# Four groups of expert tiles, late norms on VectorE, five result buffers, and the experts' first layer as three fp32r products

## What is computed

```python
x = x + tanh(g_xattn[1]) * attention16(layernorm(x), ctx)
xf = layernorm(x)                       # 2048 tokens x 128
gates = xf @ gate_w + gate_b            # 8 experts
scores, idx = top_k(gates, 2); g = softmax(scores)
for each expert e:                      # w1: 128 x 512, w2: 512 x 128
    y = gelu(xf @ w1[e] + b1[e]) @ w2[e] + b2[e]
    out += g_e * y                      # only where e is among a token's two
x = x + tanh(g_ffn[1]) * out
```

## Time and profile before

| | |
|---|---|
| median of 3 runs | 412.39 us (411.47 to 415.35) |
| profiled execution, its own time | 412.65 us |
| its span, first to last instruction | 410.9 us |
| TensorE busy (matmul) | 307.9 us, 75% |
| VectorE busy | 265.3 us, 65% |
| ScalarE busy | 198.1 us, 48% |
| GpSimd busy | 162.6 us, 40% |

### The profile page before, as it was taken

The page is one execution under the profiler, slowest core; times in us unless marked ns, Lnnn a source line. Parts: engine busy times, 40 slices in busy tenths (PEclk is TensorE's granted clock), DMA queues, the critical chain, the costliest instruction groups (busy, mean ns, idle before and its releaser), DMA issues.

```text
span 410.9 us, 7400 instructions
## 1 busy us (share of the span) xinstructions
PE 307.9 (75%) x2316; PEld 250.3 (61%) x2317; DVE 265.3 (65%) x878; ACT 198.1 (48%) x395; POOL 162.6 (40%) x289
## 2 busy tenths in 40 slices
PE   1568785271476999999999999995498999999300
PEld 0457774210333787877877787664398999999300
DVE  4647887498983978978979797855274323232162
ACT  1136664454923667666566666563153544454100
POOL 4350111450552401215272644633627644554432
PEclk9959999575557799999999999998699999999855
DMA  7434672554010111101110111005536878874171
GB/s 196 150 128 180 241 274 46 69 86 109 1 38 2 24 32 24 25 22 46 37 46 21 49 27 40 21 8 172 178 101 203 259 227 246 233 219 137 47 247 51
DMA packets 30618, 43.76 MB, mean 106 GB/s; under 512 B 5075, under 2 KB 24086, under 8 KB 30198
## 3 DMA queue, kind: packets, MB, share of 16 engines
q1 hardware_dynamic: 25798, 35.71, 30.1%
q0 software_dynamic: 3008, 6.23, 4.8%
q10 hardware_dynamic: 1776, 1.38, 1.1%
HBM read 21.99 MB, written 15.01 MB: 90 GB/s over the span
## 4 chain that ended last, share of the span: by engine, by line
PE 63%; DVE 11%; DMA 8%; issue 7%; POOL 6%; ACT 2%; DVEq 0%; SPq 0%; POOLq 0%
PE bank L1419 57%; DMA k_all<-k_hi 3%; DVE x L1390 2%; POOL k_all L315 2%; DVE nmax L1172 1%; PE bank L1734 1%; DMA xg<-sorted_rows 1%; DMA y_in<-y_rows 1%; DVE xn L919 1%; DMA sorted_rows<-token_row,place 1%; PE bank L1667 1%; POOL x L547 1%; PE bank L1445 1%; DMA x<-in_x 1%; PE bank L1679 1%
## 5 line engine op out<-in xcount | busy, mean ns | idle before, releaser
L837 ACT ACTIVATE probs<-bank 128x512 f32<-128x512 f32 x128 | 71.0, 597 | 43.9 <-PE bank L1419 43.7
L1172 DVE TENSOR_REDUCE nmax<-bank 128x2 f32<-128x512 f32 x128 | 81.7, 678 | 4.4 <-PE bank L1419 3.7
L848 ACT ACTIVATE hid<-bank,wbuf 128x256 f32<-128x256 f32 x92 | 39.6, 475 | 52.7 <-PE bank L1419 52.7
L657 POOL DMA_INDIRECT y_rows<-yout,to_row x46 | 44.0, 957 | 39.3 <-DVE yout L1379 31.4
L1419 PE MATMUL bank<-q_st,k_quad 128*128 128x256 f32 x256 | 56.0, 308 | 0.8 <-ACT probs L837 0.7
L1419 PE MATMUL bank<-k_quad,q_st 128*128 128x256 f32 x256 | 53.7, 296 | 1.6 <-ACT q_st L800 0.7
L1419 PE MATMUL bank<-xg_t,wbuf 128*128 128x256 f32 x184 | 45.3, 390 | 2.4 <-issue 1.8
L1419 PEld LDWEIGHTS bank<-q_st,k_quad 128*128 128x128 f32 x256 | 38.7, 193 | 11.9 <-ACT probs L837 11.2
L1419 PE MATMUL bank<-wbuf,hid 128*128 128x128 f32 x368 | 45.0, 275 | 0.5 <-DVE yout L1379 0.5
L1419 PEld LDWEIGHTS bank<-wbuf,hid 128*128 128x128 f32 x368 | 43.0, 192 | 0.8 <-DVE yout L1379 0.7
L1419 PEld LDWEIGHTS bank<-k_quad,q_st 128*128 128x128 f32 x256 | 40.5, 196 | 3.9 <-DVE nmax L1172 2.2
(11 more groups left out here) (237 smaller groups left out, 589.4 us busy)
## 6 DMA issues: line engine op xcount, KB each, us to landing
wbuf<-in_moe_pack SPq DMA_DIRECT2D x23, 578.0 KB, 4.1
sorted_rows<-zeros SPq DMA_DIRECT2D x15, 572.0 KB, 4.1
k_quad<-k_all SPq DMA_DIRECT2D x64, 48.0 KB
xg<-sorted_rows SPq DMA_DIRECT2D x23, 132.0 KB, 3.5
ctx_in<-in_ctx SPq DMA_DIRECT2D x8, 128.0 KB, 2.8
x<-in_x SPq DMA_DIRECT2D x4, 256.0 KB, 5.1
k_all<-k_hi SPq DMA_DIRECT2D x16, 64.0 KB
k_all<-k_lo SPq DMA_DIRECT2D x16, 64.0 KB
```

The lines of the kernel that those rows point to most:

```text
L657: pool.indirect_dma_start(out=y_rows[:, :], out_offset=bass.IndirectOffsetOnAxis(ap=to_row[n % 4][:, i:i + 1], axis=0), in_=yout[n % 3][:, ...
L837: act.activation(probs[quad % 2][:, j, :, :], bank[2 + j % 2][:, :] .rearrange("p (r s) -> p r s", r=2), ACT.Exp, scale=SC1)\
L848: act.activation(hid[n % 2][:, ch, :], bank[ch][:, 0:SLOT], ACT.Gelu, bias=wbuf[n % WB][:, B1P + ch:B1P + ch + 1]).then_inc(sem("gelued"), 1)
L1172: dve.tensor_reduce(nmax[m.par][:, gp, qt, :, j], bank[QUERY_BANKS[u % 3]][:, :].rearrange("p (r s) -> p r s", r=2), AX.X, ALU.max, negate ...
```

## The change

`PHASES` becomes four groups: three tiles after batch 4, two after batch 5, two after batch 6, 16 after batch 7. The buffers for weights, tokens and names move into the memory that is live during the attention, and the loads of the first three tiles no longer wait for the last attention. Tile 0 is turned at k = 1 of step 8 and goes through its first layer at k = 4; tiles 1 and 2 follow at k = 10, then the second layer of tile 0. VectorE takes the tokens of tile 0 at k = 2, those of tiles 1 and 2 at k = 12, weighs tile 0, and plans the third group there; the first planning moves to k = 6 of step 7.

The last norms, of batches 6 and 7, move to VectorE (`late_norm`, at k = 11); GpSimd keeps only names and root for them, and in its last round sorts batch 6 ahead of that. There are five buffers for results and seven for names instead of three and four.

The first layer's f32 product becomes three fp32r products per chunk: high weights by high tokens, high weights by low tokens, low weights by high tokens. ScalarE makes the high weights (`split_w1`), VectorE the low weights and both halves of the tokens (`take_tokens`).

```diff
-PHASES = ((0, 5), (5, 2), (7, NT - 7))
-KNOWN = (BATCH - 3, BATCH - 2, BATCH - 1)
+YB = 5
+PHASES = ((0, 3), (3, 2), (5, 2), (7, NT - 7))
+KNOWN = (BATCH - 4, BATCH - 3, BATCH - 2, BATCH - 1)
...
+        wbuf = [sb(f"wbuf{i}", [P, PACK], scope=c) for i in range(WB)]
...
-        xg_t = [sb(f"xg_t{i}", [P, SLOT], scope=d) for i in range(2)]
+        xg_hi = [sb(f"xg_hi{i}", [P, SLOT], F32R, d) for i in range(2)]
+        xg_lo = [sb(f"xg_lo{i}", [P, SLOT], F32R, d) for i in range(2)]
+        w1_hi = [sb(f"w1_hi{i}", [P, HID], F32R, d) for i in range(2)]
+        w1_lo = [sb(f"w1_lo{i}", [P, HID], F32R, d) for i in range(2)]
         hid = [sb(f"hid{i}", [P, HC, SLOT], scope=d) for i in range(2)]
...
-            sp.wait_ge(sem("attended"), 4 * BATCH)
+            first = PHASES[1][0]
             sp.wait_ge(sem("tiles_set"), 2)
-            for n in range(WB):
+            for n in range(first):
                 load_weights(n)
-            for i in range(2):
-                sp.wait_ge(sem(f"rows_sorted{i}"), 64 * 3)
...
+            sp.wait_ge(sem("rows_sorted0"), 64 * 3)
+            sp.wait_ge(sem("rows_sorted1"), 64 * 2)
+            for n in range(first):
                 load_rows(n)
-            for n in range(4, NT):
+            for n in range(first, NT):
                 if n == PHASES[1][0]:
                     sp.wait_ge(sem("tiles_set"), 4)
-                    sp.wait_ge(sem("rows_sorted2"), 64)
+                    sp.wait_ge(sem("rows_sorted1"), 64 * 3)
                 if n == PHASES[2][0]:
                     sp.wait_ge(sem("tiles_set"), 6)
+                    sp.wait_ge(sem("rows_sorted2"), 64)
...
             def fourth_norm(b):
+                if b.n >= BATCH - 2:
+                    pool.wait_ge(sem(f"rows_sorted{(b.n - 3) % 2}"), 64 * ((b.n - 3) // 2 + 1))
+                    pool.tensor_copy(token_row[b.n % 3][:, :, :, DM], row_no[:, 2 * b.n:2 * b.n + 2, :])\
+                        .then_inc(sem("rows_named"), 1)
+                    rstd_of(b.n + (LN4 + 1), mv[b.par], var_eps[b.par], rstd[b.par], 2)
+                    return
                 rows_b = token_row[b.n % 3]
...
                 pool.wait_ge(sem("placed"), b + 1)
-                pool.wait_ge(sem("rows_named"), 2 * b + 2)
+                late = max(0, b - (BATCH - 3))
+                pool.wait_ge(sem("rows_named"), 2 * b + 2 - late)
+                if late:
+                    pool.wait_ge(sem("xn4_copied"), late)
                 pool.wait_ge(sem("xn4_ready"), b + 1)
...
                 if 2 <= n < BATCH:
                     choose(pool, n - 2)
+                if n == BATCH:
+                    sort_rows(n - 2)
                 fourth_norm(Step(0, n - 1, BATCH))
-                if n >= 2:
+                if 2 <= n < BATCH:
                     sort_rows(n - 2)
...
                     if is_step(s, BATCH) and k == 4:
                         act.activation(gelu_first[:, :], eps[:, 0:1], ACT.Gelu)
+                        split_w1(0)
+                    if is_step(s, BATCH) and k == 5:
+                        split_w1(1)
+                        gelu_tile(0)
                     if is_step(s, BATCH) and k == 15:
-                        gelu_tile(0)
+                        split_w1(2)
+                        gelu_tile(1)
...
+            def split_w1(n):
+
+                act.wait_ge(sem(f"w_landed{n % WB}"), 16 * (n // WB + 1))
+                if n >= 2:
+                    act.wait_ge(sem("hid_done"), HC * (n - 1))
+                act.activation(w1_hi[n % 2][:, :], wbuf[n % WB][:, 0:HID], ACT.Copy).then_inc(sem("w1_high"), 1)
...
             unrolled(step_c, BATCH)
-            for n in range(1, NT):
+            for n in range(2, NT):
+                if n + 1 < NT:
+                    split_w1(n + 1)
...
                         halves_of(o.par, 2, o.n * SEQ)
                     if o.valid and k == 11:
                         variances_of(o.n + (LN4 + 1), o.par, 2)
+                        if is_step(o, BATCH - 2) or is_step(o, BATCH - 1):
+                            late_norm(o.n)
                     if s.valid and s.n >= 2 and k == 3:
                         top_two(s.n - 2)
                     if s.valid and s.n >= 2 and k == 13:
                         find_place(s.n - 2, bank[7])
+                    if is_step(s, BATCH - 1) and k == 6:
+                        begin_tiles(0)
                     if is_step(s, BATCH - 1) and k == 14:
-                        begin_tiles(0)
+                        begin_tiles(1)
+                    if is_step(s, BATCH) and k == 2:
+                        take_tokens(0)
                     if is_step(s, BATCH) and k == 12:
-                        take_tokens(0)
                         take_tokens(1)
-                        begin_tiles(1)
+                        take_tokens(2)
+                        weigh(0)
...
                         maximum(k - QUERY_LAG)
+
+            def late_norm(b):
+
+                late = b - (BATCH - 3)
+                dve.wait_ge(sem("rstd_done"), b + (LN4 + 1))
+                dve.wait_ge(sem("rows_named"), 2 * b + 2 - late)
+                for k, ready in ((0, "xn4_ready"), (1, "xn4_copied")):
+                    for i in range(2):
+                        ins = norm(token_row[b % 3][:, i, k, 0:DM], x[:, b * SEQ + i * P:b * SEQ + (i + 1) * P], b % 2, i)
+                    ins.then_inc(sem(ready), 1)
             def add_gate_bias(b, raw):
...
                 dve.wait_ge(sem("xg_turned"), n + 1)
                 if n >= 2:
                     dve.wait_ge(sem("hid_done"), HC * (n - 1))
-                dve.tensor_copy(xg_t[n % 2][:, :], bank[6][:, 0:SLOT]).then_inc(sem("xg_t_ready"), 1)
+                dve.tensor_copy(xg_hi[n % 2][:, :], bank[6][:, 0:SLOT]).then_inc(sem("xg_split"), 1)
+                dve.wait_ge(sem("w1_high"), n + 1)
+                dve.tensor_tensor(w1_lo[n % 2][:, :], wbuf[n % WB][:, 0:HID], w1_hi[n % 2][:, :].bitcast(F32),
+                                  ALU.subtract)
+                dve.wait_ge(sem("xg_split"), n + 1)
+                dve.tensor_tensor(xg_lo[n % 2][:, :], bank[6][:, 0:SLOT], xg_hi[n % 2][:, :].bitcast(F32),
+                                  ALU.subtract).then_inc(sem("xg_t_ready"), 1)
                 names = xg[n % 4][:, :, DM]
                 dve.scalar_tensor_tensor(spare[n % 2][:, :], names, 0.5, spare_no[:, n, :], ALU.is_lt, ALU.mult)\
...
             unrolled(step_c, BATCH)
-            for n in range(NT):
+            add_gate_bias(BATCH - 1, bank[4][:, 0:16])
+            top_two(BATCH - 1)
+            choose(dve, BATCH - 1)
+            dve.tensor_tensor(soft[:, 0, :], top[:, :, 1], top[:, :, 0], ALU.subtract).then_inc(sem("top_gap"), 1)
+            for n in range(1, NT):
                 if n + 2 < NT:
                     take_tokens(n + 2)
                 weigh(n)
-                if n == 0:
-                    add_gate_bias(BATCH - 1, bank[4][:, 0:16])
-                    top_two(BATCH - 1)
-                    choose(dve, BATCH - 1)
-                    dve.tensor_tensor(soft[:, 0, :], top[:, :, 1], top[:, :, 0], ALU.subtract).then_inc(sem("top_gap"), 1)
                 if n == 1:
...
                     if is_step(s, BATCH) and k == 0:
+                        pe.wait_ge(sem("q_shifted"), 2 * BATCH)
+                        project_gates(BATCH - 2, bank[5][:, 0:16])
+                    if is_step(s, BATCH) and k == 1:
                         pe.wait_ge(sem("s_maxed"), 16 * BATCH)
-                        project_gates(BATCH - 2, bank[0][:, 0:16])
+                        turn_tokens(0)
                     if is_step(s, BATCH) and k == 3:
-                        rank_choices(BATCH - 2, bank[1])
+                        pe.wait_ge(sem("gates_ready"), BATCH - 1)
+                        rank_choices(BATCH - 2, bank[5][:, 16:40])
+                    if is_step(s, BATCH) and k == 4:
+                        pe.wait_ge(sem("exped"), 16 * BATCH)
+                        hidden(0)
+                        turn_tokens(1)
                     if s.valid and s.n >= 2 and k == 11:
                         pe.wait_ge(sem("x3_done"), o.n + 1)
                         rank_choices(s.n - 2, bank[7])
                     if is_step(s, BATCH) and k == 10:
+                        hidden(1)
+                        turn_tokens(2)
                         pe.wait_ge(sem("rank_step"), 3 * (BATCH - 2) + 2)
-                        pe.wait_ge(sem("counted"), 2)
-                        pe.wait_ge(sem("exped"), 16 * BATCH)
-                        pe.wait_ge(sem("q_shifted"), 2 * BATCH)
-                        turn_tokens(0)
...
                         pe.wait_ge(sem("gelued"), HC * (n - 1) + ch + 1)
-                    mm(bank[ch][:, 0:SLOT],
-                       wbuf[n % WB][:, ch * P:(ch + 1) * P], xg_t[n % 2][:, :]).then_inc(sem("hid_done"), 1)
+                    cs = slice(ch * P, (ch + 1) * P)
```

(17 more changed lines are left out.)

66 lines of the change are left out of this document (29 added, 37 removed).

## The result

| | before | after |
|---|---|---|
| median of the runs on one chip | 413.87 us (4 runs, 411.47 to 416.43) | 419.98 us (4 runs, 418.67 to 422.19) |
| profiled execution, its own time | 412.65 us | 422.19 us |
| its span | 410.9 us | 420.4 us |

The changed kernel takes 1.017 times as long, 95% interval 1.0117 to 1.0222: slower, 6.1 us by the medians. The forecast was 417.5 us in a range of 411 to 423. The profiled execution of after is the longest of its four runs, so its differences from before come out larger than those of the medians.

What follows compares the result with a forecast made beforehand. TensorE's matmuls were taken to bound the full tiles, VectorE's serial list the start from the hole to tile 4's tokens. 412.65 + 10.4 (later start) - 5.2 (18 shorter periods) - 0.3 (last layer one) = 417.5 us, range 411 to 423.

Steps and rivals of the forecast that it cites:

- Layer one: Experts' tiles, TensorE: 12 products at 0.12 us make 1.44, saving 0.29 per tile, period 3.45.
- The weights: Tiles: from load wait to layer one 6.7 us against two periods of 6.9; at a landing of 4.0 just fits.
- One sign that I named: Tiles: ScalarE's split waiting for a DMA in every tile would show the forecast wrong.
- The start, batch 6: VectorE's list: first planning before x puts x 0.90 us later, at 273.8, and the gates of batch 6 1.0 later.
- the norm and the pair behind it: VectorE, batch 6: four norm pieces of 0.377 us, then find_place(5) and begin_tiles(1), 4.17 by a like pair.
- The start, batch 7: Interlocked lists: `on` 7.4 us late behind layer one of tile 0, root behind four sort issues, take_tokens(4) 9.3 late at 319.4.
- are there by about 283, ahead of need: Start: weights and rows of tiles 0 to 2 load from about 274, each weight load landing in at most 5.1 us.
- The sum: Whole kernel: 412.65 + 10.4 for the start - 5.2 over 18 periods - 0.3 in the last layer one = 417.5 us.
- the rivals: Early start faster, 402.4 (8 in 100); loss cancels gain, 412 to 413 (10); weights 423 (12); port 431 (4); dear products 438 (4).
- products 0.11 us apart: Tiles: fp32r at 0.11 gives 2 us more, part of the rival that loss and gain cancel, 412 to 413; 10 in 100.
- the dear products: Rival, tiles: layer one isn't cheaper, 0.216 us per product, 0.86 more per tile, 438 us; 4 in 100.
- The port: Rival, tiles: VectorE's weight subtraction waits up to 0.95 us for a scatter's issue, period 4.2, 431 us; 4 in 100.

Runs made afterwards that it cites:

- the runs with one edit: Changed kernel with GpSimd's root of batch 7 ahead of sorting batch 6: 417.83 us; with `on` ahead of tile 0's layer one: 415.47 us.
- the new order: Changed kernel, same work reordered: batch 7's tail first in step 8, rows loaded before weights, early tiles taken in VectorE's waits: 408.5 us, ratio 0.9854.
- the order with the third planning first: Reordered kernel (408.5 us) with third planning ahead of batch 7's gates and, up to tile 5, gelu ahead of ScalarE's split: 406.91 us, ratio 0.9836.

## Why the prediction was right

The mechanism and the direction were right: `on` behind layer one of tile 0, the root behind four sort issues, and VectorE's serial list behind both are what the rows and the runs with one edit show. Several terms of the sum were not, and they can be read one by one. By the profiled executions the difference is 9.54 us against 4.85 forecast; 1.30 of it lies ahead of the change's first effect. By the medians it is 6.1. That the time fell well inside the range owes something to luck: batch 6 was put 1 us too late, which hid part of a miss in batch 7.

**Layer one** in fp32r: 0.12 us per product and a period of 3.45 were forecast; the rows show 0.12 and 3.44. VectorE's take was put at 1.53; its three parts start 0.34 and 0.60 apart, so it takes 1.36.

**The weights** did just fit: landings from 322 to 388 us took 3.9 to 4.6, median 4.0. But 18 periods took 62.90 us, 0.98 more than 18 times 3.44, and gave 4.41 back where 5.2 was forecast. One sign that I named was badly chosen. These rows group ScalarE's splits from 322 to 390 us in after: what ended ScalarE's idle time before them (us, times), and who waited for them:

```profile
  DMA wbuf<-in_moe_pack: 26.3, 18
...
  DVE w_lo L1414: 0.8, 3
```

ScalarE's split waited for a DMA in every one of 18 tiles, which I had called a sign that the forecast is wrong. ScalarE has the time; only 3 of the waits reached VectorE, 0.8 us in all. The sign should have been VectorE waiting for ScalarE. How little room there was shows where loads landed in 5.1 and 7.1: TensorE of the new order idled there, 0.67 and 1.75 us.

**The start, batch 6**: x was forecast 0.90 late and is 0.86 net; the gates of batch 6 were forecast 1.0 late and are 0.04 net. The mis-sized terms are the norm and the pair behind it: 1.51 + 4.17 forecast, 1.03 + 3.69 measured (277.47 to 282.19). Four norms in a row overlap: 1.03 from the first to what follows them, not four times 0.377. And the 4.17 came from the pair with the last planning, which is for 16 tiles and works on 128 columns; for two tiles they are 16 columns, and it took 3.11 (279.08 to 282.19), as the first planning in the earlier trace rows.

**The start, batch 7**: `on` was forecast 7.4 late and is 9.25 net. The failed step is one sentence: weights and rows of tiles 0 to 2 "are there by about 283, ahead of need". Both halves failed. These rows of after have the loads issued from 275 to 286 us, with the median time to landing:

```profile
wbuf<-in_moe_pack SPq DMA_DIRECT2D x3, 578.0 KB, 6.2
xg<-sorted_rows SPq DMA_DIRECT2D x3, 132.0 KB, 5.4
```

The forecast had at most 5.1 for a load of weights; three in a row took 6.2. The rows of tile 0 were issued at 279.44, behind them in SyncE's queue, and TensorE's wait for them ended at 285.01, net 283.7. And 283 was not ahead of need: TensorE had been ready for k = 1 since 282.06 (285.01 - 2.95), net 280.8, which the prediction never worked out. That slot turns the rows and stands ahead of turning av, so the reciprocal came at 286.56 and inv_wide at 286.95, net 2.54 late instead of 1.0. Had the rows come at 283 net, inv_wide would still have been some 1.8 late by the same steps, an estimate from these rows. From there on the steps held: inv_wide to `on` 8.09 against 7.8 forecast, `on` to tile 1's tokens 8.51 (303.55) against 8.8. VectorE's wait for the root behind four sort issues was 3.33.

From tile 1's to tile 4's tokens it is 19.19 against 18.7, so that tile 4's, forecast at 319.4, stand at 322.74, net 321.44. TensorE's layer two of tile 0 ran at the lower clock, 3.12 us against 1.79 at the full one, and VectorE waited 1.29 for it, where the prediction had weigh(0) follow without a wait; I had taken the lower clock for layer one alone, though the granted clock stayed at 0.50 for the whole stretch from 293 to 310.

**The sum** with measured terms: 412.65 + 1.30 + 12.49 (tile 4's layer one, net) - 4.41 - 0.21 (the last layer one) = 421.8, against 422.19. None of the rivals came about: layer one of tile 0 did start 2.2 us earlier than before, but `on` behind it didn't. Two of their figures are slightly off by their own terms: products 0.11 us apart make a period of 3.33, not 3.31, and the dear products sum to 438.6. The port is refuted for the scatters: the weight subtraction at 340.75 took 0.69 inside an issue from 340.72 to 341.68, and all 23 took 0.68 to 0.70.

## What to carry to other kernels

When work is pulled forward into a hole, look at what the hole's end depends on: here `on`, the root and the rows each stood behind the work that was pulled forward, in three in-order lists, and moving it behind them turned 1.7% slower into 1.6% faster with the same work. A cheaper product whose operands must be split ahead of time moves the need for its weights forward; price the split in the stretch where it isn't covered, since here the start gave up 2.1 to 5.4 us against 0.7 to 4.5 that the tiles gave back. When work is said to be there ahead of need, work out the need as well, from the slot in the list that waits for it. And name as a sign of trouble the wait of the engine that sets the pace, not that of an engine with time to spare.

## What the runs showed of the hardware

- An fp32r product of 256 columns starts 0.12 us after the one before at a granted clock of 1.00 (331.69, 331.81, 331.93 in after) and 0.21 after it at 0.50 (305.78, 305.99, 306.20). The Trainium skill, "TensorE: Matmul & The Clock Gate", section "Wait — 56ns, not 53.3ns?", gives columns by the clock with 2.5 ns on top at the higher level. For 256 columns that makes 0.213 and 0.109, an estimate from the page's rule: the rows at 0.50 agree, those at 1.00 are 0.01 longer.
- Three loads of 578 KB issued one behind another from 275.98 on landed in 6.2 us (median), and rows of 132 KB behind them in 5.4; in the tiles of after the medians are 4.0 and 3.8.
- In the new order TensorE idled for 2.66 us at a granted clock of 1.00 and fell to the lower level only when it worked again: the next tile took 4.98 us instead of 3.44. In the order with the third planning first it idled for 1.82 at the same place, and the clock stayed at 1.00.
- VectorE's small operations are stretched threefold beside GpSimd's products. Rows of the timelines of VectorE and GpSimd in before, in step 7:

```profile
275.46 0.43 DVE L1291 SCALAR_TENSOR_TENSOR place<-top_f,rank 128x4 uint32<-128x4 f32 x1
...
276.06 0.54 DVE L1319 TENSOR_SCALAR whole<-whole 128x8 f32<-128x8 f32 x1
276.64 0.53 DVE L1321 SCALAR_TENSOR_TENSOR whole<-whole,used 128x8 f32<-128x8 f32 x1
...
275.26 0.60 POOL L585 TENSOR_TENSOR centred<-x,mv 128x256 f32<-128x256 f32 x1
...
275.97 1.18 POOL L594 TENSOR_TENSOR token_row<-centred,rstd 128x256 f32<-128x256 f32 x2
```

The three of VectorE end within 0.04 us of the ends of GpSimd's centring and of its two products (taking half of 1.18 for each). In after, where GpSimd no longer makes this norm, the same three take 0.16, 0.17 and 0.17 (at 279.00, 279.28 and 279.49). The Trainium skill, "SBUF — State Buffer", section "Who interferes with whom", says that a VectorE instruction with two SBUF inputs and a GpSimd instruction that reads SBUF exclude each other. These rows agree for the two with two inputs; the middle one has a single input, is stretched all the same, and isn't covered by that sentence. The subtraction inside a scatter's issue, above, has two inputs and was not held up.
